# Reciprocals of the softmax sums on VectorE in four pieces, keys stacked by halves, and the order of the work placed anew

## The reference, cut to what matters

```python
# block 0
_x = _group_norm(x, gn_scale, gn_bias)             # 32 groups
q, k, v = _lin_ch(_x, Wq, bq), _lin_ch(_x, Wk, bk), _lin_ch(_x, Wv, bv)   # each in 4 heads of 32
scores = jnp.einsum('bhdxy,bhdij->bhxyij', q, k) / sqrt(C)
weights = jax.nn.softmax(scores, axis=-1)          # over the 1024 keys
h = _lin_ch(jnp.einsum('bhxyij,bhdij->bhdxy', weights, v), Wp, bp)
x = (x + h) / sqrt(2.0)
# block 1
h = _group_norm(x, gn_w, gn_b)                     # 8 groups
q, k, v = jnp.split(jnp.einsum('bnc,oc->bno', h_flat, qkv_w) + qkv_b, 3, axis=-1)
attn = jax.nn.softmax(jnp.einsum('bnc,bmc->bnm', q, k) * scale, axis=-1)
out = jnp.einsum('bnc,oc->bno', jnp.einsum('bnm,bmc->bnc', attn, v), proj_w) + proj_b
return out + x
```

## Time and profile before

| | us |
|---|---|
| median of 3 runs | 1835.58 (1827.13 to 1838.28) |
| profiled execution | 1824.1, its span 1822.1 |
| TensorE busy | 1641.6 (90%), mean granted clock 0.945 |
| VectorE, ScalarE, GpSimd busy | 1133.0 (62%), 1076.8 (59%), 1096.0 (60%) |
| transfers | 120.63 MB, mean 66 GB/s |

### The profile page before, as it was taken

The page is one execution under the profiler, slowest core; times in us unless marked ns, Lnnn a source line. Parts: engine busy times, 40 slices in busy tenths (PEclk is TensorE's granted clock), DMA queues, the critical chain, the costliest instruction groups (busy, mean ns, idle before and its releaser), DMA issues.

```text
span 1822.1 us, 25657 instructions
## 1 busy us (share of the span) xinstructions
PE 1641.6 (90%) x9319; PEld 1082.2 (59%) x9319; DVE 1133.0 (62%) x1897; ACT 1076.8 (59%) x1825; POOL 1096.0 (60%) x503
## 2 busy tenths in 40 slices
PE   3889798989989898998989899998989999889978
PEld 1334365656656665665666566665656666556647
DVE  2666575756767675766767566676756666676232
ACT  1245465656656565665656566565656666556734
POOL 1077676665757666575766657477655747765720
PEclk8598899999999999999999999999999999999989
DMA  6131304140321414032140404114040411300000
GB/s 189 58 70 65 76 19 115 38 122 24 100 58 36 117 36 122 24 111 49 35 127 26 122 25 118 46 42 116 25 122 25 124 39 46 101 24 13 13 12 18
DMA packets 65837, 120.63 MB, mean 66 GB/s; under 512 B 26032, under 2 KB 26672, under 8 KB 65712
## 3 DMA queue, kind: packets, MB, share of 16 engines
q1 hardware_dynamic: 65712, 118.99, 23.3%
HBM read 76.22 MB, written 42.21 MB: 65 GB/s over the span
## 4 chain that ended last, share of the span: by engine, by line
PE 72%; DMA 11%; SPq 5%; DVE 5%; issue 3%; ACT 3%; POOL 0%; ACTq 0%; POOLq 0%; DVEq 0%
PE bank L906 13%; PE acc L846 12%; PE scores L885 11%; PE scores L828 10%; DMA k_stack<-parts_dram 9%; PE scores L872 5%; PE acc L911 3%; PE bank L911 3%; PE scores L864 3%; PE scores L865 3%; PE scores L866 3%; DVE halfmax L711 3%; SPq L432 2%; PE bank L933 2%; PE bank L915 2%
## 5 line engine op out<-in xcount | busy, mean ns | idle before, releaser
L517 POOL TENSOR_TENSOR sum<-sum,probs 128x1024 f32<-128x1024 f32 x448 | 1048.7, 2373 | 467.8 <-PE acc L846 425.0
L711 DVE TENSOR_REDUCE halfmax<-bank 128x1 f32<-128x512 f32 x1024 | 679.6, 686 | 363.7 <-PE bank L906 358.1
L553 ACT ACTIVATE probs<-scores 128x512 f32<-128x512 f32 x896 | 519.3, 600 | 458.2 <-PE scores L828 453.5
L906 PE MATMUL bank<-k_stack,q_stack 96*128 96x512 f32 x1024 | 457.3, 465 | 133.1 <-DMA k_stack<-parts_dram 104.7
L828 PE MATMUL scores<-q_stack,k_stack 97*128 97x512 f32 x1024 | 443.9, 446 | 2.3 <-DMA q_stack<-neg 2.3
L906 PEld LDWEIGHTS bank<-k_stack,q_stack 96*128 96x128 f32 x1024 | 198.4, 198 | 302.6 <-issue 179.8
L885 PEld LDWEIGHTS scores<-v,turned 128*128 128x128 f32 x1952 | 253.8, 192 | 36.9 <-ACT turned L573 17.1
L885 PE MATMUL scores<-v,turned 128*128 128x128 f32 x1952 | 260.7, 277 | 4.6 <-ACT turned L573 3.5
L846 PE MATMUL acc<-probs,v 128*32 128x512 f32 x1792 | 236.6, 642 | 0.0
L828 PEld LDWEIGHTS scores<-q_stack,k_stack 97*128 97x128 f32 x1024 | 197.0, 194 | 62.7 <-issue 37.8
L753 DVE TENSOR_REDUCE negmax<-scores 128x1 f32<-128x1024 f32 x128 | 156.5, 1222 | 59.8 <-PE scores L866 59.5
(11 more groups left out here) (86 smaller groups left out, 1318.9 us busy)
## 6 DMA issues: line engine op xcount, KB each, us to landing
q_stack<-parts_dram SPq DMA_DIRECT2D x96, 256.0 KB, 4.4
k_stack<-parts_dram SPq DMA_DIRECT2D x48, 512.0 KB, 9.4
xin<-x_dram SPq DMA_DIRECT2D x16, 512.0 KB, 3.5
x<-x_dram SPq DMA_DIRECT2D x16, 512.0 KB, 3.6
parts_dram<-q_hi SPq DMA_DIRECT2D x16, 512.0 KB, 2.6
parts_dram<-q_lo SPq DMA_DIRECT2D x16, 512.0 KB, 3.6
parts_dram<-k_hi SPq DMA_DIRECT2D x16, 512.0 KB, 2.6
parts_dram<-k_lo SPq DMA_DIRECT2D x16, 512.0 KB, 3.7
```

The lines of the kernel that those rows point to most:

```text
L517: pool.tensor_tensor(total, total, probs[:, ring_slot(i, half, kt), 2 * two:2 * two + 2, :], ALU.add).then_inc(added[two], 1)
L553: act.activation(dst, score_bank(i, index), ACT.Exp).then_inc(exp_done, 1)
L711: dve.tensor_reduce(halfmax[:, h, t, half:half + 1], banks[p][:, :], AX.X, ALU.max).then_inc(bank_free[p][VE], 1)
L906: mm = pe.matmul(dst[:, :], qs[0:SPLIT, q_half(i, arg // FIRST), h, tile(t % 4)], ks[0:SPLIT, i % 2, h, halves(half)], start=True, stop=True)
```

## The change

The reciprocals of block 0's sums are taken by VectorE in `rb` itself, on all 128 partitions, in four pieces of 128 columns per half; the transfers around them, `compact` and `recip_dram` go. A scale waits for its four pieces. The high parts are stored as soon as ScalarE has written them. The keys are stacked in two halves of 512 keys with a semaphore each, and the maxima run over the first half of the keys (for four query tiles and four heads) before the second. Queries' and keys' stores have a semaphore each. The tables have new gaps for many pieces; the last round has the reciprocals and the scale at gap 7.

```diff
@@ -55,14 +55,14 @@
-            ("rinv", t, 0, None, None, first + 3),
+            ("rinv", t, 0, None, None, first + 4),
...
-    ("out", 0, -1, GAPS + 14, None, GAPS + 14), ("out", 1, -1, GAPS + 41, None, GAPS + 41),
+    ("out", 0, -1, GAPS + 13, None, GAPS + 15), ("out", 1, -1, GAPS + 43, None, GAPS + 43),
 MAX_EARLY = (
-    18, 24, 26, 28, 29, 30, 31, 32, 33, 35, 49, 50, 51, 51, 52, 54, 56, 57, 58, 61, 62, 65, 66, 67, 68, 78, 87,
+    25, 26, 27, 27, 28, 29, 29, 32, 32, 36, 44, 46, 48, 50, 51, 53, 53, 55, 57, 58, 59, 62, 63, 66, 67, 68, 69, 75,
+    76, 78, 81, 84,
 )
 MAX_LATE = (
-    19, 26, 27, 30, 33, 34, 35, 36, 40, 41, 42, 43, 45, 46, 46, 47, 52, 52, 54, 59, 59, 62, 64, 65, 66, 68, 69, 73,
-    74, 74, 75, 77, 79, 80, 82, 83, 85,
+    18, 19, 27, 30, 30, 34, 34, 35, 36, 40, 41, 44, 47, 51, 55, 57, 59, 59, 62, 63, 64, 66, 67, 69, 70, 73, 74, 75,
+    79, 84, 85, 86,
 )
 MAX_AT = sorted([(g, 0) for g in MAX_EARLY] + [(g, 1) for g in MAX_LATE])
 EARLY_MAX = [("max", n, 1, g, None, g) for n, (g, late) in enumerate(MAX_AT) if not late]
 LATE_MAX = [("max", n, 1, g, None, g) for n, (g, late) in enumerate(MAX_AT) if late]
 SHIFTS = [
-    ("gather", 0, 1, None, None, 55), ("shift", 0, 1, 58, None, 58), ("gather", 1, 1, None, None, GAPS + 24),
+    ("gather", 0, 1, None, None, 57), ("shift", 0, 1, 58, None, 58), ("gather", 1, 1, None, None, GAPS + 27),
     ("shift", 1, 1, GAPS + 28, None, GAPS + 28),
 ]
 NEXT0 = [
-    ("stats0", 0, 2, None, None, 43), ("mean0", 0, 2, 45, None, 45), ("var0", 0, 2, 51, None, 51),
-    ("affine0", 0, 2, None, None, 62), ("norm0", 0, 2, None, GAPS + 1, None),
+    ("stats0", 0, 2, None, None, 40), ("mean0", 0, 2, 46, None, 46), ("var0", 0, 2, 50, None, 50),
+    ("affine0", 0, 2, None, None, 62), ("norm0", 0, 2, None, GAPS + 0, None),
     ("q0", 0, 2, GAPS + 5, GAPS + 5, GAPS + 6), ("q0", 1, 2, GAPS + 6, GAPS + 6, GAPS + 6),
-    ("k0", 0, 2, GAPS + 6, GAPS + 6, GAPS + 6), ("k0", 1, 2, GAPS + 7, GAPS + 7, GAPS + 7),
-    ("v0", 0, 2, GAPS + 7, GAPS + 8, None), ("v0", 1, 2, GAPS + 16, GAPS + 17, None),
+    ("k0", 0, 2, GAPS + 6, GAPS + 6, GAPS + 6), ("k0", 1, 2, GAPS + 7, GAPS + 7, GAPS + 8),
+    ("v0", 0, 2, GAPS + 7, GAPS + 8, None), ("v0", 1, 2, GAPS + 18, GAPS + 18, None),
 ]
 CHAIN = [
-    ("save", 0, 0, None, 35, None), ("sums", 0, 0, 45, 45, None), ("recip", 0, 0, None, None, 51),
-    ("scale", 0, 0, None, None, 59), ("proj", 0, 0, 61, None, 61), ("stats1", 0, 0, None, None, 61),
+    ("save", 0, 0, None, 35, None), ("sums", 0, 0, 45, 45, None), ("recip", (0, 0), 0, None, None, 46),
+    ("recip", (0, 1), 0, None, None, 50), ("recip", (0, 2), 0, None, None, 52), ("recip", (0, 3), 0, None, None, 53),
+    ("scale", 0, 0, None, None, 59), ("proj", 0, 0, 61, None, 61), ("stats1", 0, 0, None, None, 63),
     ("save", 1, 0, None, GAPS + 3, None), ("sums", 1, 0, GAPS + 6, GAPS + 6, None),
-    ("recip", 1, 0, None, None, GAPS + 13), ("scale", 1, 0, None, None, GAPS + 19),
-    ("proj", 1, 0, GAPS + 20, None, GAPS + 20), ("stats1", 1, 0, None, None, GAPS + 22),
-    ("mean1", 0, 0, GAPS + 23, None, GAPS + 23), ("var1", 0, 0, GAPS + 25, None, GAPS + 25),
-    ("affine1", 0, 0, None, None, GAPS + 26), ("norm1", 0, 0, None, GAPS + 30, None),
-    ("q1", 0, 0, GAPS + 36, GAPS + 36, GAPS + 36), ("q1", 1, 0, GAPS + 36, GAPS + 37, GAPS + 38),
-    ("k1", 0, 0, GAPS + 38, GAPS + 38, GAPS + 38), ("k1", 1, 0, GAPS + 38, GAPS + 38, GAPS + 39),
-    ("v1", 0, 0, GAPS + 38, GAPS + 39, None), ("v1", 1, 0, GAPS + 42, GAPS + 43, None),
+    ("recip", (1, 0), 0, None, None, GAPS + 9), ("recip", (1, 1), 0, None, None, GAPS + 13),
+    ("recip", (1, 2), 0, None, None, GAPS + 15), ("recip", (1, 3), 0, None, None, GAPS + 15),
+    ("scale", 1, 0, None, None, GAPS + 19), ("proj", 1, 0, GAPS + 21, None, GAPS + 21),
+    ("stats1", 1, 0, None, None, GAPS + 21), ("mean1", 0, 0, GAPS + 24, None, GAPS + 24),
+    ("var1", 0, 0, GAPS + 25, None, GAPS + 25), ("affine1", 0, 0, None, None, GAPS + 31),
+    ("norm1", 0, 0, None, GAPS + 33, None), ("q1", 0, 0, GAPS + 36, GAPS + 36, GAPS + 38),
+    ("q1", 1, 0, GAPS + 37, GAPS + 37, GAPS + 38), ("k1", 0, 0, GAPS + 38, GAPS + 38, GAPS + 38),
+    ("k1", 1, 0, GAPS + 38, GAPS + 38, GAPS + 39), ("v1", 0, 0, GAPS + 39, GAPS + 39, None),
+    ("v1", 1, 0, GAPS + 42, GAPS + 42, None),
 ]
 ROUND = folded(EARLY_MAX + BLOCK1 + VALUES + CHAIN + NEXT0 + SHIFTS + LATE_MAX)
-    ("save", 1, -1, None, 4, None), ("sums", 1, -1, 6, 6, None), ("recip", 1, -1, None, None, 8),
-    ("scale", 1, -1, None, None, 14), ("proj", 1, -1, 15, None, 15), ("stats1", 1, -1, None, None, 15),
-    ("mean1", 0, -1, 16, None, 16), ("var1", 0, -1, 17, None, 17), ("affine1", 0, -1, None, None, 19),
-    ("norm1", 0, -1, None, 19, None),
+    ("save", 1, -1, None, 4, None), ("sums", 1, -1, 6, 6, None), ("recip", (1, 0), -1, None, None, 7),
+    ("recip", (1, 1), -1, None, None, 7), ("recip", (1, 2), -1, None, None, 7), ("recip", (1, 3), -1, None, None, 7),
+    ("scale", 1, -1, None, None, 7), ("proj", 1, -1, 9, None, 9), ("stats1", 1, -1, None, None, 9),
+    ("mean1", 0, -1, 11, None, 11), ("var1", 0, -1, 12, None, 12), ("affine1", 0, -1, None, None, 14),
+    ("norm1", 0, -1, None, 14, None),
...
-        compact = sb("compact", [C // 2, 2, HEADS * KT])
-        recip_dram = nc.dram_tensor("recip_dram", (HEADS, N), F32).ap()
-        parts_out = sem("parts_out")
+        parts_out = [sem(f"parts_out_{which}") for which in "qk"]
         stacked_q = [sem(f"stacked_q{half}") for half in range(2)]
-        stacked_k = sem("stacked_k")
+        stacked_k = [sem(f"stacked_k{half}") for half in range(2)]
...
+        def max_of(n):
+
+            return n // FIRST * 4 + n // 4 % 4, n // 16 % 2, n % 4
...
             def put_parts(i):
 
                 for n, which in enumerate(("q0", "k0")):
+                    sp.wait_ge(hi_done[0], 4 * i + 2 * n + 2)
+                    sp.dma_start(parts_dram[2 * n], part[2 * n][:, :].bitcast(F32)).then_inc(parts_out[n], 16)
 
                     for piece in [(which, h, i) for h in range(2)]:
                         sp.wait_ge(bank_free[bank_of(piece)][VE], given_back(piece))
-                    for k in (2 * n, 2 * n + 1):
-                        sp.dma_start(parts_dram[k], part[k][:, :].bitcast(F32)).then_inc(parts_out, 16)
+                    sp.dma_start(parts_dram[2 * n + 1], part[2 * n + 1][:, :].bitcast(F32)).then_inc(parts_out[n], 16)
 
             def stack_queries(i, half):
-                sp.wait_ge(parts_out, 64 * (i + 1))
+                sp.wait_ge(parts_out[0], 32 * (i + 1))
                 if 2 * i + half >= 3:
 
                     sp.wait_ge(score_full, 4 * KT * (2 * i + half - 2) + (half == 0))
@@ -414,10 +419,12 @@
                                  parts_dram[k][:, halves(half)].rearrange("(h r) n -> r h n", h=HEADS)).then_inc(
                                      stacked_q[half], 16)
 
-            def stack_keys(i):
+            def stack_keys(i, half):
+                sp.wait_ge(parts_out[1], 32 * (i + 1))
                 for group, k in enumerate((2, 2, 3)):
-                    sp.dma_start(ks[DH * group:DH * (group + 1), i % 2, :, :].bitcast(F32),
-                                 parts_dram[k].rearrange("(h r) n -> r h n", h=HEADS)).then_inc(stacked_k, 16)
+                    sp.dma_start(ks[DH * group:DH * (group + 1), i % 2, :, halves(half)].bitcast(F32),
+                                 parts_dram[k][:, halves(half)].rearrange("(h r) n -> r h n", h=HEADS)).then_inc(
+                                     stacked_k[half], 16)
 
             def load_shift(i, half):
                 piece = ("shift", half, i)
@@ -425,23 +432,6 @@
                 sp.dma_start(qs[SPLIT:SPLIT + 1, q_half(i, half), :, :].rearrange(
                     "p h (t n) -> p (h t) n", n=C).bitcast(F32), neg[:, :].bitcast(F32)).then_inc(shift_loaded, 16)
-            def turn_sums(i, half):
-                piece = ("sums", half, i)
-                sp.wait_ge(bank_free[bank_of(piece)][SC], given_back(piece))
-                for h in range(HEADS):
-                    sp.dma_start(compact[:, half, KT * h:KT * (h + 1)], rb[DH * h:DH * h + 1, halves(half)].rearrange(
-                        "o (p e) -> o p e", e=KT)).then_inc(sums_in, 16)
-
-            def spread_reciprocals(i, half):
-                n = 2 * i + half + 1
-                sp.wait_ge(recip_done, n)
-                sp.dma_start(recip_dram[:, halves(half)].rearrange("h (p e) -> p h e", e=KT),
-                             compact[:, half, :].rearrange("p (h e) -> p h e", h=HEADS)).then_inc(recip_out, 16)
-                sp.wait_ge(recip_out, 16 * n)
-                for h in range(HEADS):
-                    sp.dma_start(rb[head(h), halves(half)],
-                                 recip_dram[h:h + 1, halves(half)].to_broadcast([DH, HALF])).then_inc(rb_loaded, 16)
-
...
             load_x(1)
             put_parts(0)
             stack_queries(0, 0)
-            stack_keys(0)
```

(43 more changed lines are left out.)

## The result

The changed kernel takes 2014.09 us in the median of 4 runs (2001.97 to 2018.10), the kernel before 1836.93: a ratio of 1.0963, 95% interval 1.0909 to 1.1016. The profiled execution took 2001.97 us, its span is 2000.1 us.

What follows compares the result with a forecast made beforehand. The prediction took TensorE's program as the bound. From 1824.1 us it took 85.9 (keys' waits), 37.8 (clock), 3.6 (round 0), 6 (start) and 2.2 (end), added 15 (VectorE): 1703.6, or 1714 against the median; range 1685 to 1830.

Steps and rivals of the forecast that it cites:

- the scale: VectorE's scale (L740) beside GpSimd's additions: 1.9 us for half 1, 1.3 for half 0, no cost against now.
- rival 1: GpSimd locks out the scale at gap 59 or 19: some 11 us a round, 1868; chance 0.16, few rounds 0.12.
- The keys' first half in time: Before the maxima (L906): first half lands at 1029.9, wanted at 1030.85; waits of 85.9 us and clock's 37.8 go.
- The reciprocal: On VectorE, a 128 x 128 piece takes 0.91 us by the profile's rows, 1.2 by the skill's eight steps.
- VectorE's extra work: Reciprocals add 6.6 us a round to VectorE; TensorE sees 1 us of it, 15 us over 15 rounds.
- The start: At the kernel's start, the keys' wait of 15.2 us loses 6 in all; ends 3.9 and 8.
- The sum without the scale's error: Whole kernel: the terms leave 1703.6 us of the profiled execution's 1824.1, 1714 against the median; no scale cost included.
- the 8.3 us "in one place": Of TensorE's 17.7 us of waits for a bank that VectorE still holds, 8.3 fall in one place.

Runs made afterwards that it cites:

- experiment 7: The kernel before with only the keys' part (early high-part stores, keys by halves, maxima in that order); gaps and reciprocals as before: 1813.46 us, 0.9879.
- experiment 8: The kernel before, but GpSimd waits for half 0's scale before its 23rd addition of a round: 1825.67 us, 0.9933 of the kernel before.
- experiment 1: The changed kernel, but GpSimd waits for the scale before its 6th and its 23rd addition of a round: 1684.63 us, 0.9152 of the kernel before.
- experiment 10: The kernel of experiment 1 with each reciprocal piece taken a second time into a spare tile: 1728.69 us, 0.9447 of the kernel before.
- experiment 5: The changed kernel with half 0's scale one gap earlier, 58 in place of 59: 1837.90 us, 0.9999 of the kernel before.
- experiment 6: The changed kernel, but each GpSimd addition also waits for the one just before it: 1704.98 us, 0.9280 of the kernel before.

## Why the prediction was wrong

The step that failed is the scale: "I take 1.9 for half 1 and 1.3 for half 0: no cost against now." Measured: 9.0 and 12.6 us. The mechanism stood in the text as rival 1, with its places and its price; what was wrong is the weight of the evidence. Three scales of the kernel before came into a train of additions, two got in, one did not, and I let two outvote one. The one of the earlier trace rows at the very place of the later scale, 10.4 us into a train of eight, was luck: experiments 7 and 8 have the same scale of round 15 at 8.78 and 8.77 us. For half 0 the prediction itself worked out that the scale might come behind the forming of x1, as in the earlier trace rows, and still took the 1.31 us of a scale that comes ahead of it.

The rival's price for one of the two scales was 7.6 and about 9 us of stall and 2.7 of clock; measured are 6.45 and 10.68. But it was priced for one of them, 1868 us. With both it would have been 1714 + 2 x 154 = 2022 against 2014 measured, and that this is so near is in part luck: the start of the sum, 1714, was 29 us too high (below) and the price of both, 308, was 21 too low against the 329 that the two waits gave back. The range ended at 1830 and had no place for two independent lock-outs in every round.

The other steps, read from experiment 1, where the scale can get in:
- The keys' first half in time: right, no wait in a steady round, and the clock is 1.00 as forecast. A steady round takes 96.8 us, forecast 98.
- The reciprocal: 0.93 us, forecast 0.91 from the slope of the earlier trace rows; the 1.2 us estimated from the eight steps of the Trainium skill (VectorE: DVE Perf Modes, the fixed hardware budget) is too high.
- VectorE's extra work: 1 us a round taken, none shows; experiment 10 shows that it would begin to show beyond it.
- The start: its wait fell from 15.2 to 8.9 us, 6 forecast.
- The sum without the scale's error: 1714 forecast, 1684.63 measured. 15 of the 29 us are the term for VectorE. 11 are a term that the sum left out: the 8.3 us "in one place" of the earlier trace rows are the stall behind the locked out scale of the earlier trace rows, and with the lower clock after it they cost the 11 us that experiment 8 took away. 3 us are left over.

The best version is experiment 1: 8.5% faster than the kernel before and 16% faster than the changed one.

## What to carry to other kernels

When a wait goes, ask what it kept apart. Here the wait for the reciprocals' transfers brought half 1's multiplication to GpSimd's last addition (experiment 7); without it the multiplication comes about 8 us earlier, into the middle of the train. For half 0 a shift of 0.8 us against GpSimd decides between 12.6 and 0.77 us (experiment 5). An instruction whose duration in the trace has a minimum of 0.68 and a maximum of 10.5 us is a warning worth more than its mean; look at what the other engine does in each case, and take the worst one as the price until a run shows otherwise. Where one engine locks another out, make the opening explicit with a wait, rather than rely on where the order of the work happens to leave one.

## What the runs showed of the hardware

In the changed kernel a VectorE multiplication of two SBUF operands waits, 29 times of 32, not for the one GpSimd addition that runs, but for the whole train: 12.6 us through five additions and a forming of x1, 9.0 through the rest of eight. The Trainium skill (SBUF — State Buffer, Who interferes with whom) has the later one blocked until the other finishes; experiment 6 agrees with that, with a pause of 0.17 us between additions (2.91 us at most), and the changed kernel does not, where additions follow each other without a pause (9.0 and 12.6 us).

Where the kind of instruction changes from addition to tensor_scalar, a waiting multiplication got in every time in a steady round (1.31 us before, 0.77 in experiment 5). In round 0 it did not: in the changed kernel it was asked for 0.14 us before the addition gave way and took 13.32 us, in experiment 5 it took 12.57. So the kind of boundary is not the whole rule. From tensor_scalar to addition it got in once in the changed kernel (0.99 us at 1093.67) and was locked out in the other steady rounds, also where it was asked for at the same 0.66 us into the forming (12.54 us at 1199.77). Why it gets in there once, and now and then between two additions (1.32 and 1.87 us in the earlier trace rows), stays open; no run was made for it.

The reciprocals, which read one SBUF operand, were not touched: they take 0.94 us in the median beside a busy GpSimd and beside an idle one.
